# Index columns copied one at a time on GpSimd, each beside its own gather

## The chip, the cores and the metric

One NeuronCore of one Trainium2 chip runs the program. The metric is the device time of one execution in microseconds (us), the median of the runs shown; lower is better. TensorE is called PE here, VectorE DVE, ScalarE ACT, GpSimd POOL and SyncE SP.

## The reference

A chain of four graph layers over 100000 nodes of 64 float32 features and 50000 edges. Each layer takes `h = relu(layernorm(x))` and adds its result to `x`:

```python
edge_index = jnp.stack([src, dst])
h = jnp.maximum(_layernorm(x), 0.0)
x = x + _L0_gnn_ref(h, edge_weight, edge_index, 2)      # two weighted hops: segment_sum(w * x[src], dst)
h = jnp.maximum(_layernorm(x), 0.0)
x = x + _L1_gnn_ref(h, edge_index, W, b)                # degree-normalised convolution
h = jnp.maximum(_layernorm(x), 0.0)
x = x + _L2_gnn_ref(h, edge_index, W1, b1, W2, b2)      # neighbour sums, then a two-layer MLP
h = jnp.maximum(_layernorm(x), 0.0)
x = x + _L3_gnn_ref(h, src, dst, edge_attr_32, ...)     # messages of both end nodes and edge features, MLP, sum, MLP
```

## The kernel before

The edges are sorted by destination. They lie in SBUF with 128 partitions and T = 392 columns (391 edges of a partition and one for its border). A unit is G = 14 columns, there are U = 28 units, and a step is a pair of units, b = 0 and 1, so there are STEPS = 14 steps. Rows of 64 features that belong to one column are fetched or written by one indirect DMA of POOL: 128 rows of 256 bytes, with 128 row numbers, one in each partition. So a unit costs 14 indirect DMAs, a step 28.

The program has five stages, one after the other, in each of which all engines work on the same steps:

- the first hop (`hop0` on POOL): POOL gathers rows of `x` and scatters sums with an add into two tables. The gathers of the first four units are issued ahead of everything, in the loop over `u` at the top of the diff; the later ones stand between the scatters and take their row numbers from slots that DVE fills. Those later ones are not touched
- the second hop (`hop1`): POOL scatters with an add into `xu`, 28 DMAs in a step, and gathers nothing
- the first and the second source pass, called S0 and S1 below (`for k, f in enumerate(sp_)`, the function `body`): POOL gathers 28 columns a step, from `xu` in S0 and from `tables[0]` in S1. At the same time the other engines also work through all 100000 nodes (the dense pass), independent of these gathers except for their place in each engine's order
- the last pass, called T below (`t_gather`, `t_scatter`): in a regular step POOL first scatters the 28 columns of one step to `out` and then gathers the 28 columns of the step three further on. DVE's side is `last_pass`.

Each engine has one instruction order, written out by hand, and engines wait on semaphores. The row numbers of a gather are read from a slot, `isl[b]`, a tile of 128x14 int32, and not from the large index tile. `slot_copy` is the copy of POOL that fills a slot and raises `s_slot`; `gather` then issues one indirect DMA for each column. In S0 a slot and its buffer `ga[b]` are free when DVE has centred the rows of that unit (`centred`, L2251); in S1 when DVE has added them to another tile (`ga_free`, L2227). In T DVE itself fills the slot for the next gather (`next_slots`, L2382) and only then raises `ga_free`; POOL fills it only for the first step. POOL scatters of step i (L1059) wait for `o_ready`, which DVE raises late in its pass (the profile shows it as "DVEq L80"), and every following gather of POOL stands behind them in its order.

Of the kernel before, what the change touches and what calls it, by code (L numbers as in the profile page):

```python
# [14 lines left out]
G = 14  # L15
U = T // G
STEPS = U // 2
# [140 lines left out]
def gnn(nc, x, src, dst, edge_attr, edge_weight, W1g, b1g, W2a, b2a, W2b, b2b, mW1, mb1, mW2, mb2, uW1, ub1,  # L158
        uW2, ub2, out):
    ctx = ExitStack()  # L160
    with ctx:
# [10 lines left out]
        tables = [dram(f"table{k}", [ROWS + P, D]) for k in range(2)]  # L172
# [49 lines left out]
        dstc_i = sb("dstc_i", [P, T], I32)  # L222
        ptr_i = sb("ptr_i", [P, T], I32)
# [15 lines left out]
        hin, xw, h, vt, ga = (pair(n, unit) for n in ("hin", "xw", "h", "vt", "ga"))  # L239
# [5 lines left out]
        us = pair("us", unit)  # L245
# [24 lines left out]
        isl, osl = (pair(n, [P, G], I32) for n in ("isl", "osl"))  # L270
        isl_of = [*isl, *pair("isl_ahead", [P, G], I32)]
# [18 lines left out]
        ga_of = [*(t[:, :, :] for t in ga), ccu[0][2], ccu[1][2]]  # L290
# [90 lines left out]
        s_slot = sem("pool_slot_copied")  # L381
# [26 lines left out]
        B2K = [0, 1]  # L408
# [451 lines left out]
        def _(pool):  # L860
# [62 lines left out]
            def slot_copy(o, i_):  # L923

                return nc.gpsimd.tensor_copy(o, i_).then_inc(s_slot, 1)

            def gather(o, table, idx, s, columns=range(G)):
                for g in columns:
                    nc.gpsimd.indirect_dma_start(  # L929
                        o[:, g, :], None, table, bass.IndirectOffsetOnAxis(idx[:, g:g + 1], 0)).then_inc(s, 16)  # L930


            after.wait_ge(s_node, 1)
            base = 0

            hop_max, all_max = pool.to_reg(ROWS + 4 * P - 1), pool.to_reg(ROWS + N + 4 * P - 1)
            f = hops[0]
            for u in range(4):  # L940
                slot_copy(isl_of[u][:, :], dstc_i[:, u * G:u * G + G])
                after.wait_ge(s_slot, base + u + 1)
                gather(ga_of[u], x, isl_of[u], f.got[u])
            base += 4

            def hop0(i):
                for b in B2K:
# [60 lines left out]
            for k, f in enumerate(sp_):  # L1008
                if k == 0:
                    table, index = xu, u_i  # L1010
                else:
                    table, index = tables[k - 1], ptr_i
                    for b in B2K:
                        after.wait_ge(sp_[0].kept[b], 2 * 16 * STEPS)

                def body(i, first):
                    for n, b in enumerate(B2K if k == 0 else B2K[::-1]):
                        if not first:

                            if k == 0:  # L1020
                                after.wait_ge(*f.centred.at(i - 1, ("l", b)))
                            else:
                                after.wait_ge(*f.ga_free.at(i - 1, ("g", b)))
                        slot_copy(isl[b][:, :], index[:, bass.ds(ecol(i, b), G)])
                        after.wait_ge(s_slot, base + 2 * i + n + 1)
                        gather(ga[b], table, isl[b], f.got[b])

                for i in range(STEPS):
                    body(i, i == 0)
                base += 2 * STEPS  # L1030
# [12 lines left out]
            def t_gather(i, first=False):  # L1043
                for b in B2K:
                    if not first:
                        after.wait_ge(*tt.ga_free.at(i - 1, ("g", b)))
                    if first:
                        slot_copy(isl[b][:, :], ptr_i[:, bass.ds(tcol(i, b), G)])
                        after.wait_ge(s_slot, base + b + 1)
                    gather(ga[b], tables[1], isl[b], tt.got_a[b])  # L1050

            def t_scatter(i, first=False):
                for b in B2K:
# [8 lines left out]

            for q in LANES:
                after.wait_ge(s_dense[q], 16 * DSTEPS)
            t_gather(0, True)
            t_gather(1)
            t_gather(2)
            t_scatter(0, True)
            t_gather(3)
            for i in range(2, STEPS - 2):  # L1070
                t_scatter(i - 1)
                t_gather(i + 2)
            for i in (STEPS - 3, STEPS - 2):
                t_scatter(i)

# [681 lines left out]
        def _(dve):  # L1757
# [619 lines left out]

            descending = range(G - 1, -1, -1)

            def next_slots(n, b):  # L2380
                n = 0 if isinstance(n, int) and n == STEPS else n
                return V.tensor_copy(isl[b][:, :], ptr_i[:, bass.ds(tcol(n, b), G)])  # L2382

            def last_pass(i, first=False, more_steps=True):
                if i is not None:
                    own.step(i)
# [47 lines left out]
                if more_steps:  # L2434
                    hd = layer_norm(own, tt, j, "d1", B2K, [full(gx[b]) for b in B2K], [full(xw[b]) for b in B2K],
                                    [[(tt.load_x[b], 32 * (j + 1))] for b in B2K],
                                    scale=lambda b: dis_d[:, bass.ds(tcol(j, b), G)])
                    for b in B2K:
                        own.wait(hd[b], (tt.load[b], 16 * 6 * (j + 1)))
                        hd[b] = own.did(V.tensor_tensor(full(xw[b]), full(xw[b]), full(a3[b]), ALU.add))  # L2440
                    for b in B2K:
                        own.wait(hd[b])
                        settled(dve, j)
                        tt.rows.raise_by(V.tensor_tensor(full(xw[b]), full(xw[b]), cols(dis_d, tcol(j, b)), ALU.mult), ("vd", b))

                    for b in B2K:
                        own.wait((tt.got_a[b], 16 * G * (j + 1)))
                        tt.rows.raise_by(V.tensor_tensor(full(us[b]), full(hin[b]), full(ga[b]), ALU.add), ("us", b))
                    for b in B2K:
                        next_in = own.did(next_slots(j + 1, b))  # L2450
                        own.wait(tt.rows.at(j, ("us", b)), next_in)
                        tt.ga_free.raise_now(dve, ("g", b))

                aggregate(0)
# [122 lines left out]
            def first_step():  # L2577
# [69 lines left out]
                    own.wait((tt.got_a[b], 16 * G), (tt.load[b], 16 * 6))  # L2647
                    tt.rows.raise_by(V.tensor_tensor(full(us[b]), full(hin[b]), full(ga[b]), ALU.add), ("us", b))
                for b in B2K:
                    next_in = own.did(next_slots(1, b))  # L2650
                    own.wait(tt.rows.at(0, ("us", b)), next_in)
# [66 lines left out]
```

## Time and profile before

| | |
|---|---|
| median of 3 runs | 4624.67 us (4622.48 to 4624.89) |
| span of the profiled execution | 5754.7 us |
| span minus median | 1130.0 us |
| first hop and what is ahead of it | 0 to about 1210 us |
| second hop | about 1210 to 2130 us |
| S0 | about 2130 to 3068 us |
| S1 | about 3068 to 4002 us |
| T | about 4002 us to the end |
| indirect DMAs of POOL | 2760 of its 2843 instructions |

The profiled execution's only time is its span; nothing is given for it outside the span. It is longer than the runs that are timed, so a duration in it is read as that of a profiled execution, and where the two must differ is a question of its own. In the rows, "idle before" is the time in which an engine did nothing before an instruction, and the name behind the arrow is what released it: "issue" is nothing that the profile shows, "remote" an update for which the profile has no instruction that ended at that time.

### The profile page before, as it was taken

The numbers are of one execution on the slowest core, as the hardware profiler recorded it, in microseconds if no ns is written. First come the engines' busy times: TensorE is split into PE (matmuls) and PEld (weight loads), VectorE is DVE, ScalarE is ACT, GpSimd is POOL, SyncE is SP. The second block draws the span as 40 slices with busy tenths as digits, with TensorE's granted clock in tenths as the row PEclk, the third lists the DMA queues.
The fourth block names the chain that finished last, engine by engine and source line by source line (L and its number), as shares of the span: only waits on it lengthen the run. The fifth ranks groups of instructions, "written<-read, shape, count | busy, mean of one in ns | idle before, by whom it ended". The sixth has DMA issues, their size and how long they took to land. (4 is left out here: it accounts for less than half of the span.)

```text
span 5754.7 us, 60611 instructions
## 1 busy us (share of the span) xinstructions
PE 3759.0 (65%) x18706; PEld 3006.2 (52%) x18706; DVE 3033.3 (53%) x7288; ACT 2016.3 (35%) x5132; POOL 3313.7 (58%) x2843
## 2 busy tenths in 40 slices
PE   3776666676999975565556777763566655666665
PEld 2544444446898964444445555553454444455454
DVE  4644444455556546665665766755454434455442
ACT  2444444451111113443444444431233333333332
POOL 4888888887888874444332554553444554445544
PEclk7776666675555557887888777875778877777787
DMA  8333333334444432222222333333121111121110
GB/s 293 51 51 51 51 51 51 51 42 73 87 81 87 87 40 82 78 93 79 96 77 75 108 125 123 112 107 130 54 91 55 59 57 57 54 91 55 60 54 21
DMA packets 335488, 452.10 MB, mean 79 GB/s; under 512 B 208111, under 2 KB 233301, under 8 KB 334740
## 3 DMA queue, kind: packets, MB, share of 16 engines
q1 hardware_dynamic: 159268, 361.69, 17.8%
q0 software_dynamic: 176000, 87.72, 12.5%
q8 instruction: 109, 1.79, 0.1%
q14 instruction: 111, 0.91, 0.1%
HBM read 258.41 MB, written 225.53 MB: 84 GB/s over the span
## 5 line engine op out<-in xcount | busy, mean ns | idle before, releaser
L929 POOL DMA_INDIRECT ga<-table,isl x784 | 783.9, 1000 | 278.1 <-issue 231.3
L1059 POOL DMA_INDIRECT out_x<-acc,osl x392 | 430.0, 1097 | 755.6 <-DVEq L80 640.4
L997 POOL DMA_INDIRECT xu<-acc,osl x392 | 625.1, 1595 | 144.6 <-issue 103.1
L1205 PE MATMUL tp<-xw,cc 128*128 128x394 f32 x784 | 411.5, 623 | 345.8 <-DVE cc L2011 215.4
L1242 PE MATMUL tp<-us,wide 128*128 128x64 f32 x1568 | 416.8, 422 | 87.4 <-DVE us L2139 49.2
L929 POOL DMA_INDIRECT ga<-xu,isl x392 | 394.0, 1005 | 121.5 <-issue 116.5
L1205 PEld LDWEIGHTS tp<-xw,cc 128*128 128x128 f32 x784 | 141.5, 220 | 603.1 <-issue 325.4
L1093 PE MATMUL mm<-ident,wide 128*128 128x128 f32 x1176 | 213.1, 343 | 355.6 <-DVE wide L2218 275.7
L1242 PEld LDWEIGHTS tp<-us,wide 128*128 128x128 f32 x1568 | 380.0, 332 | 92.2 <-DVE us L2139 49.4
L1255 PE MATMUL tp<-acc,wide 128*128 128x64 f32 x1560 | 423.3, 427 | 0.8
L1093 PEld LDWEIGHTS mm<-ident,wide 128*128 128x128 f32 x1176 | 180.0, 182 | 406.1 <-issue 323.2
L1255 PEld LDWEIGHTS tp<-acc,wide 128*128 128x128 f32 x1560 | 372.0, 329 | 20.8 <-ACT acc L1558 5.6
L1190 PE MATMUL tp<-us,wide 128*128 128x64 f32 x1568 | 341.0, 421 | 59.0 <-DVE us L1928 59.0
L960 POOL DMA_INDIRECT hop_even<-acc,osl x196 | 321.9, 1642 | 99.5 <-issue 57.3
L1190 PEld LDWEIGHTS tp<-us,wide 128*128 128x128 f32 x1568 | 336.6, 332 | 64.8 <-issue 64.8
L960 POOL DMA_INDIRECT hop_odd<-acc,osl x196 | 321.6, 1641 | 60.8 <-issue 57.3
L1558 ACT ACTIVATE acc<-tp,h 128x64 f32<-128x64 f32 x392 | 102.0, 311 | 691.7 <-PE tp L1255 536.6
L2461 DVE SCALAR_TENSOR_TENSOR mean_row<-st,mm 128x14 f32<-128x14 f32 x26 | 4.4, 168 | 587.3 <-remote 549.1
L1128 PE MATMUL mm<-bias,rows 128*128 128x455 bf16 x392 | 158.7, 405 | 228.2 <-issue 77.0
L1100 PE MATMUL mm<-cc,u1s 128*128 128x512 f32 x448 | 249.9, 691 | 76.0 <-ACT zx L1593 50.5
L1523 ACT ACTIVATE hin<-tp,xw 128x391 bf16<-128x391 f32 x392 | 233.1, 595 | 133.7 <-PE tp L1205 88.3
L1093 PE MATMUL tp<-ident,us 128*128 128x128 f32 x392 | 75.1, 360 | 312.3 <-ACT eft L1697 257.0
(378 smaller groups left out, 9513.8 us busy)
## 6 DMA issues: line engine op xcount, KB each, us to landing
wide<-xu SPq DMA_DIRECT2D x84, 448.0 KB
zx<-key_rows SPq DMA_DIRECT2D x28, 896.0 KB
out_x<-wide SPq DMA_DIRECT2D x56, 448.0 KB, 3.4
table<-acc SPq DMA_DIRECT2D x56, 448.0 KB, 2.5
xf<-xs SPq DMA_DIRECT2D x56, 448.0 KB
wide<-table SPq DMA_DIRECT2D x56, 448.0 KB
xu<-in_x SPq DMA_DIRECT2D x25, 1000.0 KB
hop_even<-zeros SPq DMA_DIRECT2D x1, 12544.0 KB
```

What stands on the lines that cost most here:

```text
L929: nc.gpsimd.indirect_dma_start(o[:, g, :], None, table, bass.IndirectOffsetOnAxis(idx[:, g:g + 1], 0)).then_inc(s, 16)
L960: nc.gpsimd.indirect_dma_start(hop[odd], bass.IndirectOffsetOnAxis(osl[b][:, g:g + 1], 0), acc[b][:, g, :], None, compute_op=ALU.add).then ...
L997: nc.gpsimd.indirect_dma_start(xu, bass.IndirectOffsetOnAxis(osl[b][:, g:g + 1], 0), acc[b][:, g, :], None, compute_op=ALU.add).then_inc(f ...
L1059: nc.gpsimd.indirect_dma_start(out, bass.IndirectOffsetOnAxis(osl[b][:, g:g + 1], 0), acc[b][:, g, :], None, bounds_check=nodes_max, oob_i ...
L1093: t = nc.tensor.transpose(o[0:w, j * P:j * P + P], blk, ident[:, :])
L1100: t = nc.tensor.matmul(o[:, c:c + n], weights, flat(src_)[:, c:c + n], start=True, stop=extra is None)
L1128: nc.tensor.matmul(o[:, at:at + HB * C], rows3[:, :], bias[:, k, 0:HB * C], start=True, stop=False)
L1190: t = nc.tensor.matmul(o[:, g * D:g * D + D], equal[b][:, c, (g % 2) * P:(g % 2) * P + P], us[b][:, c, :], start=n == 0, stop=n == 1)
L1205: f.key_row.raise_by(nc.tensor.matmul(tp[1][:, at:at + KEYS], reach[:, g * P:g * P + P], key_steps, start=True, stop=True), ("g", b, g))
L1242: t = nc.tensor.matmul(o, equal_run[:, 2 * q + n, mine:mine + P], us[b][:, 2 * q + n, :], start=n == 0, stop=alone and n == 1)
L1255: t = nc.tensor.matmul(o, equal_run[:, c, 2 * P + mine:3 * P + mine], passed[:, c, :], start=False, stop=n == 1)
L1523: nc.scalar.activation(sign_out[:, 2 * (g % 2), 0:EC], tp[1][:, at + 3:at + KEYS], ACT.Sign, bias=key_high[:, column], scale=-1.0, accum_o ...
```

## The change

A new helper, `gather_by_column`, takes the place of the pair of one slot copy and one `gather` of 14 columns. For each column g it copies one column of the index tile (128x1) into column g of the slot, waits until that copy has raised `s_slot`, and issues the gather of that column. It serves the four units ahead of the first hop, S0, S1 and all of T. In T POOL now copies for every step, so DVE's `next_slots` copies (28 of them) and its wait on them go away; `ga_free` still waits for DVE's sum. The number of gathers, their order, their tables and their buffers stay as they are.

```diff
+            def gather_by_column(o, table, slot, index, c, s, copied):
+                for g in range(G):
+                    slot_copy(slot[:, g:g + 1], index[:, c + g:c + g + 1])
+                    after.wait_ge(s_slot, copied + g + 1)
+                    gather(o, table, slot, s, (g,))
+                return copied + G
...
             for u in range(4):
-                slot_copy(isl_of[u][:, :], dstc_i[:, u * G:u * G + G])
-                after.wait_ge(s_slot, base + u + 1)
-                gather(ga_of[u], x, isl_of[u], f.got[u])
-            base += 4
+                copied = gather_by_column(ga_of[u], x, isl_of[u], dstc_i, u * G, f.got[u], copied)
...
-                        slot_copy(isl[b][:, :], index[:, bass.ds(ecol(i, b), G)])
-                        after.wait_ge(s_slot, base + 2 * i + n + 1)
-                        gather(ga[b], table, isl[b], f.got[b])
+                        copied = gather_by_column(ga[b], table, isl[b], index, ecol(i, b), f.got[b], copied)
...
-            def t_gather(i, first=False):
+            def t_gather(i, copied, first=False):
                 for b in B2K:
                     if not first:
                         after.wait_ge(*tt.ga_free.at(i - 1, ("g", b)))
-                    if first:
-                        slot_copy(isl[b][:, :], ptr_i[:, bass.ds(tcol(i, b), G)])
-                        after.wait_ge(s_slot, base + b + 1)
-                    gather(ga[b], tables[1], isl[b], tt.got_a[b])
+                    copied = gather_by_column(ga[b], tables[1], isl[b], ptr_i, tcol(i, b), tt.got_a[b], copied)
+                return copied
...
-            def next_slots(n, b):
-                n = 0 if isinstance(n, int) and n == STEPS else n
-                return V.tensor_copy(isl[b][:, :], ptr_i[:, bass.ds(tcol(n, b), G)])
...
                     for b in B2K:
-                        next_in = own.did(next_slots(j + 1, b))
-                        own.wait(tt.rows.at(j, ("us", b)), next_in)
+                        own.wait(tt.rows.at(j, ("us", b)))
                         tt.ga_free.raise_now(dve, ("g", b))
```

## Rows read from the trace of the kernel before

**Rows 1.** The page: the span.

```profile
span 5754.7 us, 60611 instructions
```

**Rows 2.** Groups of POOL's instructions by line: busy us, mean ns, idle before.

```profile
L929 POOL DMA_INDIRECT ga<-table,isl x784 | 783.9, 1000 | 278.1 <-issue 231.3 <-DVEq L80 39.8 <-POOL isl L925 7.1
L925 POOL COPY isl<-ptr_i 128x14 int32<-128x14 int32 x30 | 9.4, 312 | 352.0 <-DVE us L2227 349.4 <-DMA table<-fix 2.5
L925 POOL COPY isl<-map_idx 128x14 int32<-128x14 int32 x28 | 6.3, 225 | 339.5 <-DVE xc L2251 338.3 <-DMA xu<-hsum 1.2
...
L2707 POOL MEMSET const-float32-0.0<- 128x1 f32 x1 | 0.1, 104 | 0.3 <-issue 0.3
```

**Rows 3.** Whom DVE waited for, in S0, S1 and T: us, times, longest.

```profile
DVE mean_row L2208 <- remote: 191.3, 14, 20.4
DVE wide L2218 <- remote: 76.2, 11, 16.1
...
DVE wide L2218 <- remote: 151.7, 12, 13.7
DVE xw L2240 <- remote: 38.8, 8, 14.9
...
DVE mean_row L2461 <- remote: 549.1, 20, 48.6
```

**Rows 4.** Stretches of ten steps of S0, ten of S1, eight of T.

Columns: stretch, length, then busy us (instructions) of PE, PE's weight loads, DVE, ACT and POOL, granted PE clock, DMA share, GB/s.

```profile
2309.00:2953.00 644.00, 368.81 (x1982) 282.48 (x1981) 405.88 (x721) 266.73 (x561) 284.42 (x301) 0.80 0.27 86
3231.00:3846.00 615.00, 448.25 (x2480) 356.59 (x2480) 425.27 (x721) 285.12 (x582) 301.41 (x300) 0.80 0.36 119
4444.00:5428.00 984.00, 585.85 (x3504) 476.97 (x3504) 455.76 (x960) 339.06 (x625) 461.89 (x448) 0.78 0.20 63
```

**Rows 5.** POOL in order of time, S0, between the two units of a step.

```profile
2327.37 0.94 POOL L929 DMA_INDIRECT ga<-xu,isl  x1 [0.30 <-issue]
2328.31 0.21 POOL L925 COPY isl<-map_idx 128x14 int32<-128x14 int32 x1
2328.80 0.98 POOL L929 DMA_INDIRECT ga<-xu,isl  x1 [0.27 <-issue]
```

**Rows 6.** The same place in S1: DVE's instruction and POOL's copy.

```profile
3188.49 1.09 DVE L2200 SCALAR_TENSOR_TENSOR wide<-wide,st 128x896 f32<-128x896 f32 x1
...
3189.17 0.46 POOL L925 COPY isl<-ptr_i 128x14 int32<-128x14 int32 x1
```

**Rows 7.** Around the end of one gather burst of T, in order of time.

```profile
4886.77 0.95 POOL L929 DMA_INDIRECT ga<-table,isl  x1 [0.30 <-issue]
4894.19 0.17 DVE L2461 SCALAR_TENSOR_TENSOR mean_row<-st,mm 128x14 f32<-128x14 f32 x1 [8.73 <-remote]
4936.12 1.64 POOL L1059 DMA_INDIRECT out_x<-acc,osl  x1 [48.40 <-DVEq L80]
```

**Rows 8.** One burst of S0 with DVE's next start; first copy of one of S1.

```profile
2309.04 0.20 POOL L925 COPY isl<-map_idx 128x14 int32<-128x14 int32 x1 [24.23 <-DVE xc L2251]
2345.84 0.95 POOL L929 DMA_INDIRECT ga<-xu,isl  x1 [0.30 <-issue]
2349.48 1.09 DVE L2218 TENSOR_TENSOR wide<-wide,mm 128x896 f32<-128x896 f32 x1 [11.28 <-remote]
...
3231.24 0.20 POOL L925 COPY isl<-ptr_i 128x14 int32<-128x14 int32 x1 [23.66 <-DVE us L2227]
```

**Rows 9.** Late in T: the first scatter after a step without a gather burst.

```profile
5637.43 1.61 POOL L1059 DMA_INDIRECT out_x<-acc,osl  x1 [44.36 <-DVEq L80]
```

**Rows 10.** Ahead of the first hop: two DVE instructions, then POOL's first scatter.

```profile
89.86 1.28 DVE L2011 TENSOR_SCALAR cc<-mm,small 128x1024 f32<-128x1024 f32 x1 [28.24 <-remote]
104.62 1.02 DVE L2011 TENSOR_SCALAR cc<-mm,small 128x768 f32<-128x768 f32 x1 [13.48 <-remote]
138.23 1.63 POOL L960 DMA_INDIRECT hop_even<-acc,osl  x1 [40.13 <-ACT acc L1536]
```

**Rows 11.** DVE's slot copies in T: ns min/median/max, first and last start.

```profile
L2382 DVE COPY isl<-ptr_i x28: 163/171/175, 4058.2 to 5574.1; 128x14 int32<-128x14 int32 x28
```

More of the change, by code:

```diff
@@ L930, in gather @@
                         o[:, g, :], None, table, bass.IndirectOffsetOnAxis(idx[:, g:g + 1], 0)).then_inc(s, 16)
+            def gather_by_column(o, table, slot, index, c, s, copied):
[4 more added lines that the diff above has]
+                return copied + G
             after.wait_ge(s_node, 1)
-            base = 0
+            copied = 0
             hop_max, all_max = pool.to_reg(ROWS + 4 * P - 1), pool.to_reg(ROWS + N + 4 * P - 1)
@@ L1014, in _, with body @@
                         after.wait_ge(sp_[0].kept[b], 2 * 16 * STEPS)
-                def body(i, first):
-                    for n, b in enumerate(B2K if k == 0 else B2K[::-1]):
+                def body(i, first, copied):
+                    for b in B2K if k == 0 else B2K[::-1]:
                         if not first:
@@ L1023, in body @@
                                 after.wait_ge(*f.ga_free.at(i - 1, ("g", b)))
-                        slot_copy(isl[b][:, :], index[:, bass.ds(ecol(i, b), G)])
-                        after.wait_ge(s_slot, base + 2 * i + n + 1)
-                        gather(ga[b], table, isl[b], f.got[b])
+                        copied = gather_by_column(ga[b], table, isl[b], index, ecol(i, b), f.got[b], copied)
+                    return copied
                 for i in range(STEPS):
-                    body(i, i == 0)
-                base += 2 * STEPS
+                    copied = body(i, i == 0, copied)
                 for b in B2K:
@@ L1046, in t_gather @@
                         after.wait_ge(*tt.ga_free.at(i - 1, ("g", b)))
-                    if first:
-                        slot_copy(isl[b][:, :], ptr_i[:, bass.ds(tcol(i, b), G)])
-                        after.wait_ge(s_slot, base + b + 1)
-                    gather(ga[b], tables[1], isl[b], tt.got_a[b])
+                    copied = gather_by_column(ga[b], tables[1], isl[b], ptr_i, tcol(i, b), tt.got_a[b], copied)
+                return copied
             def t_scatter(i, first=False):
@@ L1064, in _ @@
                 after.wait_ge(s_dense[q], 16 * DSTEPS)
-            t_gather(0, True)
-            t_gather(1)
-            t_gather(2)
+            copied = t_gather(0, copied, True)
+            copied = t_gather(1, copied)
+            copied = t_gather(2, copied)
             t_scatter(0, True)
-            t_gather(3)
+            copied = t_gather(3, copied)
             for i in range(2, STEPS - 2):
                 t_scatter(i - 1)
-                t_gather(i + 2)
+                copied = t_gather(i + 2, copied)
             for i in (STEPS - 3, STEPS - 2):
@@ L2649, in first_step @@
                 for b in B2K:
-                    next_in = own.did(next_slots(1, b))
-                    own.wait(tt.rows.at(0, ("us", b)), next_in)
+                    own.wait(tt.rows.at(0, ("us", b)))
                     tt.ga_free.raise_now(dve, ("g", b))
```

## Prediction

> **What bounds the kernel now.** I read the page for the span, then POOL's groups by line, then the waits of DVE, then stretches of regular steps, and last single bursts in order of time. The first thing to see is that the profiled execution is not the timed one: its span is 5754.7 us [rows 1], the median of the runs 4624.67 us, 1130.0 us less. What the change costs depends on which time is missing from the timed runs.
>
> Two readings close that gap. By the first, DVE's waits on "remote" are in the profiled execution alone. They come to 267.5 us in S0, 190.5 us in S1 and 549.1 us in T [rows 3], together 1007 us, and 5754.7 - 1007 = 4748 us, within 123 us of the median. In each of these waits no instruction in the profile ended when DVE went on; DVE goes on only when POOL's burst of gathers has ended: 6.5 us after it in T (the last gather ends at 4887.72, DVE starts at 4894.19) [rows 7], 2.7 us after it in S0 (2346.79 to 2349.48) [rows 8]. I call such a wait a hold. By the second reading the holds are in the timed runs too, and POOL is quicker there: 1130 / 2760 indirect DMAs = 0.41 us each, of the 1.25 us that one takes from start to start. The first is likelier, since it needs one effect of a size that the trace itself shows, and the second needs a third off every DMA.
>
> Without holds a regular step is shorter. S0: 644 / 10 = 64.4 us [rows 4] less 267.5 / 14 = 19.1 us gives 45.3 us, with DVE busy for 40.6 us. S1: 61.5 less 190.5 / 14 = 13.6 gives 47.9 us, with DVE busy for 42.5 us. T: 984 / 8 = 123.0 us less 549.1 / 11 = 49.9 us (eleven steps have a gather burst beside a full pass) gives 73.1 us, with PE busy for 73.2 us and DVE for 57.0 us. POOL works in a step of T for 123.0 - 48.4 = 74.6 us, and waits for DVE's `o_ready` in the rest [rows 7]. So without holds POOL is as late as the others in T. Against this stands the one step of T that has a full pass and no gather burst: POOL's scatters take 39.4 us (74.6 less a gather burst of 35.0, 28 by 1.25) and it then waits 44.36 us [rows 9], 83.8 us in all, in which the other engines were not held. The step of T in the timed runs lies between 74.6 and 83.8 us. As the timed median is 123 us below my sum without holds, I take it near the low end, 75.6 us.
>
> In the two hops POOL has the longest work, but their inner gathers are not changed.
>
> **The price of one column.** Before, a gather follows another after 0.95 + 0.30 = 1.25 us. Where a slot copy stands between two gathers, the copy starts the moment the gather ends, takes 0.21 us, and the next gather starts 0.27 us after it: 2328.80 - 2327.37 = 1.43 us [rows 5]. The new code makes this pattern at every column, so a column costs 0.18 us more. The trace shows no copy of 128x1. From below, a POOL instruction of 128x1 takes 0.104 us [rows 2], which would leave 0.18 - 0.11 = 0.07 us. From above, a copy that stood beside a two-operand instruction of DVE took 0.46 us and ended when DVE's did (3189.63 and 3189.58) [rows 6]: 0.43 us more for such a column. The copies from `map_idx` average 0.225 us and those from `ptr_i` 0.312 us [rows 2], so where DVE is busy I use 0.28 us as the upper price. I take 0.18 us, as copies that meet nothing take 0.2 us with 14 columns, and the fixed part is most of it.
>
> The Trainium skill ("SBUF — State Buffer", section "SBUF: two separate sides") speaks against this change: a GpSimd instruction that reads SBUF and a DVE instruction with two SBUF inputs take the same port pair as an exclusive lock, and the later one blocks until the first is through. The copy of 0.46 us agrees. By that rule each of the some 1170 new copies is a new occasion to stand behind DVE, and if all did, the price would be that of rival 3.
>
> **Part by part.**
>
> 1. Ahead of the first hop: 56 columns by 56 copies in place of 4, so 52 by 0.18 = 9.4 us on POOL. The first scatter comes at 138.23, 40.13 us after the early gathers ended at 98.10; but 28.24 and 13.48 us of DVE's time ahead of it are holds, of which the second ends at 104.62, 6.5 us after POOL's burst [rows 10]. Without these 41.7 us the sums for the scatter would be there at 96.5, before POOL is free. So POOL's burst is on the path there, and the hop after it is POOL's own: +9.4 us.
>
> 2. S0: 28 copies a step in place of 2, 26 by 0.18 = 4.7 us, at 0.28 us 7.3 us. POOL's burst is 2309.04 to 2346.79, 37.8 us, and I let the rows be in place 2.7 us later, at the latest when DVE went on [rows 8]: 40.5 us of a step of 45.3. What hides the change is this 4.8 us; it is used up at 0.18 us and short by 2.5 us at 0.28 us. If it is short, `source_mean` of DVE is late, and the dense pass behind it in DVE's order too. Between 0 and 2.5 by 13 steps = 33 us; I take 0.8 us a step, 10 us.
>
> 3. S1: the burst is 61.5 - 23.7 = 37.8 us [rows 4, 8], with 2.7 us 40.5 of 47.9: 7.4 us of cover for 4.7 to 7.3 us. Taken as 0.
>
> 4. T: DVE's 28 copies of 0.17 us [rows 11] go, and 28 copies a step on POOL come, 5.0 us at 0.18 us. POOL's wait on a copy holds up its gathers, and behind them the scatters of the next step. POOL's step goes from 74.6 to 79.6 us; from a step of 75.6 us that is +4.0 us, by 11 steps +44 us. At a step of 83.8 us it is nothing. The three early gather bursts of T have POOL waiting for DVE behind them, so they are hidden. `ga_free` is raised some 0.3 us sooner, for nothing as DVE then waits for ACT's and PE's products anyway; where DVE or PE is the bound it is a gain of at most 28 by 0.17 = 4.8 us.
>
> Semaphore traffic and DMA: no transfer is added, and the gathers are the same ones in the same order.
>
> Sum: 9.4 + 10 + 0 + 44 = 63 us; 4624.67 + 63 = 4688 us. Against the profiled execution, where the holds end with the bursts, everything is serial: 9.4 + 13 by 4.7 twice (122) + 11 by 5.0 (55) = 187 us, with 0.28 us in S0 and S1 254 us. The span should be 5942 to 6009 us.
>
> **Rivals.**
>
> 1. Hidden. The step of T is near 83.8 us, or POOL is a little quicker when not profiled (0.07 us a DMA would account for 110 of the 123 us in the two hops alone). For it: the unheld step of rows 9. Against it: the sum of rows 3, which the median undercuts. Time: 4624.67 within 9 us, 0.2%, which is about what a measurement of this kernel can tell from no change.
>
> 2. The holds are real in the timed runs. Then every burst is on the path, as in the profile: +187 to +254 us, 4812 to 4879 us. For it: the holds end so strictly with the bursts. Against: a third off every DMA of POOL.
>
> 3. Most copies stand behind DVE, 0.43 us a column. S0: 26 by 0.43 = 11.2 less 4.8 cover, by 13 = 83 us; S1: 11.2 less 7.4, by 13 = 49 us; T: 74.6 + 12.0 - 75.6 = 11.0 by 11 = 121 us; with 52 by 0.43 = 22 us ahead, +275 us, 4900 us. Against: the copies of S0 that met DVE's reduces took 0.20 us.
>
> 4. Faster. If holds are real, they come with the rate at which gathers are issued: 28 gathers at 1.43 us instead of 1.25 us are a rate 13% lower. A hold of 49.9 us a step of T that shrinks by 13% gives back 6.5 us for the 5.0 us that the burst is longer: it decides from 10% on. By 11 steps -17 us, with the same in S0 and S1 (19.1 and 13.6 us a step, where it does not pay) at best a fall of the whole to about 4600 us. For it: holds appear only under dense gathers. Against: in the hops, where POOL never pauses, PE goes on nonetheless.
>
> **Chances.** The forecast (some 10 to 120 us slower) 0.50; hidden 0.27; rival 2 0.10; rival 3 0.04; faster 0.09. The point is the forecast's own, 4688 us. The range reaches from 4612 us, which holds the hidden case with a small gain, to 4790 us, which holds the T step at 0.28 us a column (74.6 + 7.8 - 74.6 by 11 = 86 us), S0's 33 us, S1's few us and the 15 us ahead (52 by 0.28). Left out are rivals 2 and 3 and two thirds of the faster case, 0.20. The forecast's own range is 4635 to 4745 us. Faster by over 0.2% 0.09; within 0.2% 0.22, since a part of the hidden case still pays the 9.4 us ahead of the first hop; slower 0.69.
>
> **What the changed kernel's profile would show.** Copies of 128x1 of about 0.2 us, over 1230 of them; from gather to gather 1.43 us in T and 1.45 to 1.55 us in S0 and S1; T's regular step 128 us, with POOL's wait before L1059 still 48 us; S0's and S1's steps 5 to 8 us longer; no L2382-like copy on DVE. If POOL's waits shrink by what its bursts grow, the price is hidden even there, and rival 1 is right. If DVE's "remote" waits shrink, rival 4 has its mechanism. Wrong would make me above all a copy of one column that is much cheaper or dearer than 0.2 us, and a step of T in the timed runs that POOL does not set.

## The result, and the profile after

The changed kernel takes 4806.07 us (median of 4 runs, 4793.73 to 4812.52), the kernel before 4624.78 us (4 runs): a ratio of 1.0388 [1.0372, 1.0404], 181 us slower. The forecast was 4688 us, slower, in 4612 to 4790 us. The sign held; the time lies above the range.

The page of the kernel after: span, busy time, and the chain that ended last.

```profile
span 4791.4 us, 61753 instructions
...
PE 3584.7 (75%) x18706; PEld 2876.9 (60%) x18706; DVE 3036.1 (63%) x7260; ACT 2010.5 (42%) x5132; POOL 3707.0 (77%) x4013
...
POOL 40%; issue 13%; PE 8%; DVE 6%; DMA 3%; ACT 1%; DVEq 0%; SPq 0%; POOLq 0%; ACTq 0%
```

The span is 963 us shorter than that of [rows 1], though the kernel is slower. No DVE wait on "remote" as in [rows 3] is left, and POOL no longer waits for `o_ready` in the steps of T (the 48.40 us of [rows 7] are gone). So this profile can't be laid beside the profile before. What it needs is an execution of the unchanged stages without those waits; the run `only_ahead` below gives one.

POOL's groups of the kernel after: busy us, mean ns, idle before. They answer to [rows 2].

```profile
L929 POOL DMA_INDIRECT ga<-table,isl x784 | 825.2, 1053 | 224.7 <-POOL isl L925 212.8
...
L929 POOL DMA_INDIRECT ga<-xu,isl x392 | 426.8, 1089 | 111.9 <-POOL isl L925 106.5
...
L925 POOL COPY isl<-ptr_i 128x1 int32<-128x1 int32 x784 | 225.5, 288 | 43.1 <-DVE us L2228 32.3
```

POOL's instructions on `isl` in the kernel after: ns min/median/max.

```profile
L925 POOL COPY isl<-ptr_i x784: 181/194/1132, 2825.4 to 4623.7; 128x1 int32<-128x1 int32 x196
```

POOL of the kernel after in order of time: in S1, with the instruction of DVE that the copy meets, then in T, undisturbed. They answer to [rows 5, 6].

```profile
3018.20 1.09 DVE L2201 SCALAR_TENSOR_TENSOR wide<-wide,st 128x896 f32<-128x896 f32 x1
3018.32 1.01 POOL L925 COPY isl<-ptr_i 128x1 int32<-128x1 int32 x1
3019.61 0.97 POOL L929 DMA_INDIRECT ga<-table,isl  x1 [0.27 <-POOL isl L925]
...
4253.87 1.01 POOL L929 DMA_INDIRECT ga<-table,isl  x1 [0.27 <-POOL isl L925]
4254.89 0.19 POOL L925 COPY isl<-ptr_i 128x1 int32<-128x1 int32 x1
4255.35 0.97 POOL L929 DMA_INDIRECT ga<-table,isl  x1 [0.27 <-POOL isl L925]
```

The undisturbed pattern is the one foreseen: a gather of 0.97 to 1.01 us, a copy of 0.19 us, 0.27 us idle, 1.45 to 1.48 us for a column. The mean is another matter. The median copy takes 194 ns and the mean copy 288 ns: some take up to 1.13 us. In S0, S1 and T 188 of the 1176 copies take over 0.3 us, and each of these ends within 0.08 us of the end of a DVE instruction that reads two tiles in SBUF, as the one at 3018.32 does (3019.33 and 3019.29). Beside a DVE instruction of the same length whose second input is `mm`, which TensorE wrote, a copy stays short; this is one of 77 such copies, in S0:

```profile
2128.69 1.08 DVE L2211 TENSOR_TENSOR wide<-wide,mm 128x896 f32<-128x896 f32 x1
2129.29 0.19 POOL L925 COPY isl<-map_idx 128x1 int32<-128x1 int32 x1
```

### The profile page after: what moved, and what is told of

Its sections match the earlier page's. It is cut to its first block, busy times and chain, and to the rows that moved or that the text cites. A ratio compares the mean times of both kernels' runs of the same rounds, so it can differ in the third digit from the quotient of the medians.

```text
span 4791.4 us, 61753 instructions
## 1 busy us (share of the span) xinstructions
PE 3584.7 (75%) x18706; PEld 2876.9 (60%) x18706; DVE 3036.1 (63%) x7260; ACT 2010.5 (42%) x5132; POOL 3707.0 (77%) x4013
## 4 chain that ended last, share of the span: by engine, by line
POOL 40%; issue 13%; PE 8%; DVE 6%; DMA 3%; ACT 1%; DVEq 0%; SPq 0%; POOLq 0%; ACTq 0%
POOL ga L929 22%; POOL out_x L1060 9%; POOL isl L925 6%; POOL xu L1002 4%; PE tp L1256 2%; PE tp L1243 2%; DMA xu<-acc,osl 2%; PE mm L1101 2%; PE mm L1120 1%; DVE xf L1945 1%; DVE wide L2104 1%; DVE acc L1945 1%; PE mm L1132 1%; PE mm L1094 0%; DVE wide L2099 0%
## 5 line engine op out<-in xcount | busy, mean ns | idle before, releaser
L929 POOL DMA_INDIRECT ga<-table,isl x784 | 825.2, 1053 | 224.7 <-POOL isl L925 212.8
L929 POOL DMA_INDIRECT ga<-xu,isl x392 | 426.8, 1089 | 111.9 <-POOL isl L925 106.5
L1101 PE MATMUL mm<-cc,u1s 128*128 128x512 f32 x448 | 215.7, 608 | 104.3 <-ACT zx L1594 83.0
L1094 PE MATMUL mm<-ident,wide 128*128 128x128 f32 x1176 | 191.6, 314 | 109.6 <-DVE wide L2201 59.9
L1537 ACT COPY acc<-tp 128x896 f32<-128x896 f32 x28 | 25.3, 905 | 574.9 <-DMA hop_even<-acc,osl 287.4
L925 POOL COPY isl<-ptr_i 128x1 int32<-128x1 int32 x784 | 225.5, 288 | 43.1 <-DVE us L2228 32.3
L1094 PEld LDWEIGHTS mm<-ident,wide 128*128 128x128 f32 x1176 | 161.5, 167 | 148.8 <-DVE wide L2201 79.1
```

The source lines that it names most:

```text
L929: nc.gpsimd.indirect_dma_start(o[:, g, :], None, table, bass.IndirectOffsetOnAxis(idx[:, g:g + 1], 0)).then_inc(s, 16)
L1094: t = nc.tensor.transpose(o[0:w, j * P:j * P + P], blk, ident[:, :])
L1101: t = nc.tensor.matmul(o[:, c:c + n], weights, flat(src_)[:, c:c + n], start=True, stop=extra is None)
```

## The experiments

In the kernels below the line numbers are some ten higher than in the kernel after. They ran on four chips, and the chips fall into two kinds. On two the unchanged kernel takes 4620 to 4624 us, as it did beside the result above; on the other two it takes 5829 and 5831 us, in timed runs. I call them quiet chips and holding chips. One of the quiet chips was used at two times and was quiet at both; no holding chip was, so it is likely, and not shown, that the chip decides and not the moment. The unchanged kernel's runs on the same chip stand beside each result.

### The unchanged kernel on a holding chip (control)

> The kernel before, unchanged, for its profile. Theory 1 (the holds on DVE belonged to that one profiled execution): a span of about 4622 us, near its time, T's regular step 76 us. Theory 2 (the profiled execution of this kernel always has them, and the column copies take them away): a span near 5755 us.

5820.14 us, with a span of 5817.8 us; the median of 13 runs there is 5828.88 us. Whom DVE waited for:

```profile
DVE mean_row L2461 <- remote: 512.1, 12, 49.9
DVE mean_row L2208 <- remote: 269.7, 15, 23.4
...
DVE wide L2218 <- remote: 125.3, 23, 12.5
```

These are the holds of [rows 3], in an execution whose span and time agree within 3 us. On a quiet chip the two agree as well (span 4618.7 us of 4621.03 us, next experiment). So profiling neither makes the holds nor lengthens the run, and neither theory is right as it was put: the span is long, but the timed runs there are as long. The profile before most likely came from a holding chip and its timed runs from a quiet one; which chip it was isn't recorded.

### One stage at a time, on quiet chips

The kernel before, with `gather_by_column` in one place only and this in the others; in `only_t` also without DVE's slot copies:

```diff
+            def gather_unit(o, table, slot, index, c, s, copied):
+                slot_copy(slot[:, :], index[:, c:c + G])
+                after.wait_ge(s_slot, copied + 1)
+                gather(o, table, slot, s)
+                return copied + 1
```

> The column copies only in the four units ahead of the first hop, 14-column copies elsewhere. Theory 1 (POOL's early burst is on the path): 52 more copies at some 0.18 us, +9 us, about 4634 us. Theory 2 (the first scatter waits for the other engines anyway): 4625 us.

> The column copies only in S0. Theory 1 (POOL is the bound of a step in S0 when the kernel is timed, and a column costs what the changed kernel's trace shows, 1.64 us from gather to gather in place of 1.31): up to 28 x 0.33 = 9 us a step, less what slack there was; +45 to +100 us. Theory 2 (the prediction's: DVE sets the step of S0, POOL has 4.8 us of cover): +10 us or less.

> The column copies only in S1. Theory 1 (as in S0): +40 to +90 us. Theory 2 (the prediction's: 7.4 us of cover in a step): 0 us.

> The column copies only in the last pass, DVE's slot copies gone. Theory 1 (POOL's 28 scatters and 28 gathers set the step, which is 83.5 us in the changed kernel against some 76 us): +70 to +90 us. Theory 2 (S0 and S1 cost nothing, so all of the +181 us is here): +165 to +175 us.

> The column copies in S0 and S1 alone, the rest as before. On a chip without holds: the sum of the two measured alone, +38 and +48, so +86 us, if the stages are independent. On a chip with holds: theory 1 (wider spaced gathers end the holds of S0 and S1 completely, as in the trace of the changed kernel there): 14 steps by 18 us and 14 by 14 us less, some -430 us, 5400 us, with T's 125 us a step as before. Theory 2 (what ends them is elsewhere, in T's move of the copy from DVE): within 2% of the kernel before.

| | us | before | ratio | us more | forecast |
|---|---|---|---|---|---|
| only_ahead | 4622.18 | 4624.43 | 1.0000 [0.9990, 1.0009] | 0 | 9.4 |
| only_s0 | 4662.26 | 4624.43 | 1.0085 [1.0068, 1.0102] | 38 | 10 |
| only_s1 | 4672.25 | 4624.43 | 1.0106 [1.0089, 1.0123] | 48 | 0 |
| only_t | 4713.72 | 4624.43 | 1.0200 [1.0183, 1.0217] | 89 | 44 |
| s0_and_s1 | 4711.42 | 4622.67 | 1.0190 [1.0177, 1.0204] | 89 | 10 |

The four single stages sum to 175 us of the 181. S0 and S1 together cost what they cost alone (38 + 48 = 86). Of what was expected before these runs, S1's and T's theory 1 held; S0's theory 1 was too high (at least 45, measured 38), and ahead of the first hop theory 2 held. The trace of `only_ahead` serves from here as the profile of the stages before: its S0, S1 and T are unchanged, and its time is.

Regular steps of S0 (5), S1 (8) and T (6) in `only_ahead`; columns as in [rows 4], to which they answer:

```profile
2423.30:2645.70 222.40, 170.52 (x992) 130.72 (x991) 201.96 (x361) 133.04 (x281) 152.37 (x150) 0.92 0.39 125
2957.20:3312.80 355.60, 305.10 (x1984) 247.74 (x1984) 336.62 (x577) 226.19 (x465) 251.36 (x240) 0.96 0.50 166
3845.10:4300.90 455.80, 403.53 (x2639) 326.58 (x2639) 343.92 (x722) 253.91 (x469) 353.39 (x336) 0.95 0.33 101
```

The same of the kernel after: 4, 8 and 6 steps.

```profile
2397.00:2585.00 188.00, 137.93 (x794) 106.08 (x793) 163.25 (x289) 106.29 (x226) 153.11 (x224) 0.90 0.37 118
3053.80:3435.00 381.20, 317.30 (x1984) 260.25 (x1984) 340.42 (x577) 227.52 (x464) 315.97 (x448) 0.92 0.47 153
3874.80:4375.80 501.00, 408.19 (x2633) 329.05 (x2631) 342.79 (x710) 253.47 (x470) 400.17 (x505) 0.91 0.30 92
```

A step goes from 44.5 to 47.0 us in S0, from 44.4 to 47.6 us in S1, from 76.0 to 83.5 us in T. POOL's busy time in a step of T goes from 58.9 to 66.7 us, 7.8 us for a step that is 7.5 us longer; DVE's stays at 57 us. PE's clock falls a little, from 0.95 to 0.91 of full speed; PE's busy time in a step of T grows by less than 1 us, so this is not what the step waits for.

Two of POOL's groups in `only_ahead`, and below them two of its waits (us, times, longest):

```profile
L929 POOL DMA_INDIRECT ga<-table,isl x784 | 815.0, 1040 | 247.9 <-issue 230.2 <-DVEq L80 9.6 <-POOL isl L925 8.1
...
L971 POOL DMA_INDIRECT hop_even<-acc,osl x196 | 321.9, 1642 | 81.5 <-issue 56.1 <-DMA xu<-ga 22.1 <-ACT acc L1546 3.4
```

```profile
POOL isl L925 <- DVE us L2237: 94.0, 13, 43.6
...
POOL isl L925 <- DVE xc L2261: 66.5, 12, 8.0
```

Whom DVE waited for in the kernel after (in `only_ahead` these two come to 11.9 us in 2 waits and 2.4 us in one):

```profile
DVE us L2228 <- DMA ga<-table,isl: 52.7, 13, 15.8
...
DVE st L2245 <- DMA ga<-xu,isl: 36.9, 13, 8.6
```

The direction has turned. Before, POOL waited for DVE's buffer once a step: 66.5 / 12 = 5.5 us in S0, and (94.0 - 43.6) / 12 = 4.2 us in S1 without the first. That is the cover, and after the change it is used up: DVE waits for the gathers in every step.

The price of a column comes out of the two groups of `table` gathers, per gather: 1.053 - 1.040 more for the gather, (224.7 - 247.9) / 784 = -0.030 for the idle time before it, and 0.288 for the copy, together 0.27 us. Of this, 0.19 - 0.03 + 0.03 (a gather of 974 ns in the median in place of 944) is the undisturbed 0.19 us; the rest, near 0.08 us, comes from copies that were stretched to as much as 1.13 us. The stages differ: the mean copy takes 276 ns in S0, 327 ns in S1 and 248 ns in T. A step's 28 gathers with what stands between them, from the start of the first to the end of the last (median of twelve steps), go from 38.7 to 46.0 us in S0, from 39.5 to 47.4 us in S1 and from 35.9 to 43.8 us in T.

Ahead of the first hop the 52 copies are hidden. In `only_s1`, where that part is unchanged, the first scatter's group reads:

```profile
L971 POOL DMA_INDIRECT hop_even<-acc,osl x196 | 321.5, 1640 | 90.8 <-issue 56.1 <-DMA xu<-ga 31.4 <-ACT acc L1546 3.4
```

Its wait for stored rows ("DMA xu<-ga") is 31.4 us there and 22.1 us in `only_ahead`: the 9.3 us are what POOL's burst has grown.

### The copy's place and number, on a quiet chip

All are the kernel after with another helper. `copies_first_3` issues 14 copies of one column, then one wait, then the 14 gathers. `copy_ahead_3` issues the copy of the next column ahead of a gather, so a gather waits for an older copy:

```diff
+                for g in range(G + 1):
+                    if g < G:
+                        slot_copy(slot[:, g:g + 1], index[:, c + g:c + g + 1])
+                    if g:
+                        after.wait_ge(s_slot, copied + g)
+                        gather(o, table, slot, s, (g - 1,))
```

`copied_twice` makes each copy a second time into a tile that nothing reads (two lines of its loop, set against those of `gather_by_column`):

```diff
                     slot_copy(slot[:, g:g + 1], index[:, c + g:c + g + 1])
+                    slot_copy(second_slot[:, g:g + 1], index[:, c + g:c + g + 1])
-                    after.wait_ge(s_slot, copied + g + 1)
+                    after.wait_ge(s_slot, copied + 2 * g + 2)
```

`t_pool_unit` uses `gather_unit` everywhere: one copy of 14 columns, made by POOL in T too. `direct_3` has no slots at all in the places of the change; the gathers read `index[:, c + g:c + g + 1]`.

> The 14 copies of 128x1 of a unit first, one wait, then its 14 gathers; wanted for a chip where the kernel before takes 4624 us. Theory 1 (the copy's own time on POOL is the price): +100 us or more. Theory 2 (the chain of copy, semaphore and gather at every column is the price): +50 us or less. On a chip with holds: about 5580 us, as before.

> The copy for column g + 1 ahead of the gather of column g; wanted for a chip where the kernel before takes 4624 us. Theory 1 (the copy's own time is the price): +170 us, as the changed kernel. Theory 2 (the wait on it is about half of the price): +60 to +110 us. On a chip with holds: about 5555 us.

> The changed kernel with a second copy of 128x1 at each column, of the same row numbers into a tile that nothing reads; the gather waits for both. On a chip without holds: theory 1 (a copy costs its own 0.19 us and waits behind DVE, POOL is the bound in S0, S1 and T): 1232 more copies, some 0.1 to 0.2 us each, +110 to +240 us on the changed kernel, 4920 to 5050 us. Theory 2 (the semaphore round trip is the price and a second copy passes under it): within 60 us of the changed kernel. On a chip with holds: S0 and S1 longer by the copies, T's holds shorter again, or not, if the rate of the gathers has nothing to do with them.

> 14-column copies everywhere, as before, but in T they are POOL's for every step in place of DVE's. On a chip without holds: theory 1 (POOL sets T's step): 2 x 0.18 us by 11 to 14 steps, +4 to +6 us, the part of +89 us that comes from moving the copy to POOL. Theory 2 (the move to POOL itself is dear, the gather waits there for a copy behind the scatters): +20 us or more. On a chip with holds: within 1% of the kernel before.

> No slots in the changed places, the gathers take their row numbers from the index tile. On a chip without holds: theory 1 (a gather costs the same from either tile; S0 and S1 have some 5 us a step in which POOL waits for DVE, so their slot copies were hidden, and T had them on DVE): within 9 us of the kernel before. Theory 2 (POOL's copies in S0 and S1 are paid): -10 us. On a chip with holds, as measured twice: the time of the kernel before.

| | us | before | ratio | us more | step of T |
|---|---|---|---|---|---|
| direct_3 | 4620.57 | 4622.67 | 0.9997 [0.9988, 1.0006] | 0 | 76.1 |
| t_pool_unit | 4630.88 | 4620.39 | 1.0022 [1.0013, 1.0032] | 10 | 77.5 |
| copy_ahead_3 | 4712.62 | 4620.39 | 1.0198 [1.0181, 1.0215] | 92 | 80.9 |
| copies_first_3 | 4720.76 | 4620.39 | 1.0219 [1.0202, 1.0236] | 100 | 82.1 |
| after | 4806.07 | 4624.78 | 1.0388 [1.0372, 1.0404] | 181 | 83.5 |
| copied_twice | 4955.62 | 4620.39 | 1.0728 [1.0710, 1.0746] | 335 | 88.0 |

The step of T is the mean of six, from first scatter to first scatter. Of what was expected, theory 1 held for `copies_first_3`, `copied_twice` and `direct_3` and theory 2 for `copy_ahead_3`; `t_pool_unit` fell between its two.

POOL in order of time, T: `copies_first_3`, then `copy_ahead_3`, then `copied_twice`.

```profile
4263.74 2.45 POOL L925 COPY isl<-ptr_i 128x1 int32<-128x1 int32 x14
4266.46 1.00 POOL L929 DMA_INDIRECT ga<-table,isl  x1 [0.27 <-POOL isl L925]
4267.76 0.96 POOL L929 DMA_INDIRECT ga<-table,isl  x1 [0.30 <-issue]
```

```profile
4271.72 0.19 POOL L925 COPY isl<-ptr_i 128x1 int32<-128x1 int32 x1
4272.07 0.97 POOL L929 DMA_INDIRECT ga<-table,isl  x1 [0.15 <-POOL isl L925]
```

```profile
4253.28 0.21 POOL L926 COPY isl<-ptr_i 128x1 int32<-128x1 int32 x1
4253.45 0.17 POOL L926 COPY second_slot<-ptr_i 128x1 int32<-128x1 int32 x1
4253.89 0.97 POOL L930 DMA_INDIRECT ga<-table,isl  x1 [0.27 <-POOL second_slot L926]
```

Fourteen copies back to back take 2.45 us, 0.175 us each, and one wait of 0.27 us serves 14 gathers. Made so, the copies cost 100 us of the 181. The other 81 us are what it adds to have each copy beside its own gather. These are the two groups of `copies_first_3` to set beside those of the kernel after:

```profile
L929 POOL DMA_INDIRECT ga<-table,isl x784 | 824.8, 1052 | 237.5 <-issue 222.3 <-POOL isl L925 15.2
...
L925 POOL COPY isl<-ptr_i 128x1 int32<-128x1 int32 x784 | 139.9, 234 | 54.0 <-DVE us L2242 48.2 <-DVEq L80 3.2 <-DMA table<-fix 2.5
```

The gathers take the same, 824.8 and 825.2 us, and POOL's idle time before them is even shorter in the kernel after (224.7 us in place of 237.5; 247.9 in `only_ahead`): the wait behind each copy takes the place of the 0.30 us that lie between two gathers anyway. The copies differ: the same 784 keep POOL busy for 225.5 us one by one and for 139.9 us in rows of 14 (the mean of 234 ns counts the overlap of neighbours twice). 188 copies take over 0.3 us in the kernel after and 74 here, a row of 14 giving DVE one occasion to be in its way and single copies fourteen.

Taking the gather off its own copy (`copy_ahead_3`) cuts the idle time from 0.27 to 0.15 us, below the usual 0.30 us, and the cost to 92 us, though 212 of its copies take over 0.3 us. A second copy of each column adds another 335 - 181 = 154 us, 0.125 us for each of the 1232. `direct_3` says what the slots are worth on a quiet chip: nothing, neither way. So no version here beats the kernel before there. Moving the copy of 14 columns from DVE to POOL in T costs 10 us by itself: POOL's copies from `ptr_i` come to 19.1 us in `t_pool_unit` and to 9.3 us in `only_ahead`.

### The same kernels on holding chips

`copies_first`, `copy_ahead` and `direct` are the kernels just described, run twice each; `after_again` is the changed kernel.

> Everywhere where the changed kernel copies by column: the 14 copies of 128x1 of a unit first, one wait, then its 14 gathers. As many copies, no wait between them. Theory 1 (the price of a column is the copy's own time on POOL, some 0.2 to 0.3 us, wherever it stands): about 4800 us, as the changed kernel. Theory 2 (the price is that a copy, its semaphore and the next gather form one chain at every column, which leaves nothing of the 0.30 us between two gathers to hide in): copies back to back take perhaps 0.1 us each, so some 1.4 us a unit in place of 3.9: 4680 us or less.

> As the changed kernel, but the copy for column g + 1 is issued ahead of the gather of column g, so that the gather's wait has been met long before. Theory 1 (the copy's own time is the price): about 4800 us. Theory 2 (the wait is the price: the gather can't be issued until the copy's update has come back): the copy sits in the 0.30 us between two gathers and the kernel comes back to 4625 to 4700 us.

> No slots in the changed places: each gather takes its 128 row numbers from the column of the index tile itself (the places are written out, so their columns are constants). Same rows gathered. Theory 1 (POOL is the bound in T, and a unit's 14-column copy costs 0.18 us there only if POOL does it): within 10 us of the kernel before. Theory 2 (a gather that reads a column of a tile with 392 columns is slower than one that reads a slot): slower by some 1230 x the difference.

> The 14 copies of 128x1 of a unit first, one wait, then its 14 gathers; wanted on a chip where the kernel before takes 4624 us. Theory 1 (the copy's own time on POOL is the price, 0.19 us by 14 in place of one of 0.2): 1204 copies, in T 28 by 0.19 = 5.3 us a step and nearly as much in S0 and S1, so +100 us or more. Theory 2 (the chain of copy, semaphore and gather is the price): copies back to back at 0.1 us, +50 us or less.

> The copy for column g + 1 ahead of the gather of column g; wanted on a chip where the kernel before takes 4624 us. In the trace of the other chip the gathers of T then follow each other in 1.37 us, against 1.24 there and 1.43 by the changed kernel's pattern. Theory 1 (the copy's own time is the price): +170 us as the changed kernel. Theory 2 (half of the price is the wait): +60 to +110 us.

> No slots in the changed places, the gathers take their row numbers from the index tile; wanted on a chip where the kernel before takes 4624 us. Theory 1 (a gather costs the same from either tile; POOL is the bound in T, where the kernel before has no copies on POOL): within 9 us of the kernel before. Theory 2 (POOL is the bound in S0 and S1 too): 26 to 28 steps with 2 copies less at 0.18 us, -10 us.

> The changed kernel itself, beside the kernel before on one chip. In the four runs before this the kernel before took 5829 us on another chip, with the holds of its first profile, against 4624 us. Theory 1 (there are chips with holds and chips without; the price of the change is POOL's only where there are none): where the kernel before takes 4624 us, +181 us; where it takes 5829 us the rarer gathers shorten the holds, and the changed kernel is faster, some 5500 to 5600 us. Theory 2 (the two times are a matter of the moment and not of the chip): both kernels change together within the rounds.

| | us | before | ratio |
|---|---|---|---|
| direct | 5830.93 | 5828.88 | 0.9996 [0.9974, 1.0019] |
| direct_2 | 5832.59 | 5830.65 | 1.0004 [0.9987, 1.0022] |
| copies_first | 5590.62 | 5828.88 | 0.9580 [0.9530, 0.9630] |
| copies_first_2 | 5578.91 | 5830.65 | 0.9577 [0.9555, 0.9598] |
| copy_ahead | 5552.06 | 5828.88 | 0.9519 [0.9486, 0.9552] |
| copy_ahead_2 | 5555.22 | 5830.65 | 0.9530 [0.9507, 0.9552] |
| after_again | 5234.99 | 5830.65 | 0.8986 [0.8965, 0.9006] |

On such a chip the change makes the kernel 10% faster, 5235 us where theory 1 expected 5500 to 5600. Taking the slots away does nothing here either, and copies in rows of 14 already gain 4%, but hardly in T: there, with the gathers of a unit still 1.25 us apart, the steps of `copies_first` are 122.8 us, and those of `copy_ahead`, 1.39 us apart, 124 to 126 us, against 123 to 125 us in `control`. Their gain is in S0 and S1 (from the first gather to the border sum `hsum`, from 943 and 933 us in `control` to 801 and 893 us in `copies_first`, 849 and 780 us in `copy_ahead`). Whom DVE waited for in `after_again`; no other hold is among its ten longest waits:

```profile
DVE mean_row L2457 <- remote: 350.1, 20, 40.5
```

Steps of S0 (2), S1 (8) and T (9) in `after_again`, columns as in [rows 4]:

```profile
2404.00:2499.50 95.50, 69.43 (x397) 53.69 (x397) 81.43 (x145) 53.09 (x113) 75.66 (x112) 0.89 0.37 116
3072.20:3459.80 387.60, 318.30 (x1989) 260.40 (x1990) 341.56 (x578) 226.36 (x464) 322.33 (x448) 0.92 0.45 150
3845.60:4898.40 1052.80, 660.45 (x3942) 534.07 (x3942) 511.06 (x1063) 382.37 (x703) 578.76 (x756) 0.80 0.22 66
```

A step of S0 is 47.8 us here and 64.4 us in [rows 4], of S1 48.5 and 61.5 us: near the steps of a quiet chip (47.0 and 47.6 us). A step of T is 117 in place of 123 us, 105 to 108 us in every third and 122 to 123 us in the others; there the holds are only shorter. In T the gathers are mostly 1.43 us apart, 1.49 us on average; in S0 and S1, with DVE beside them, 1.63 and 1.73 us. This distance is in part a result: where DVE isn't held, it works beside POOL and stretches the copies.

What a hold is can be read from one place in T. In `only_ahead` on a quiet chip, PE's last matmul of a unit and DVE's next instruction:

```profile
4396.88 0.33 PE L1143 MATMUL mm<-wg,vt 128*128 128x65 f32 x2
...
4397.24 0.17 DVE L2471 SCALAR_TENSOR_TENSOR mean_row<-st,mm 128x14 f32<-128x14 f32 x1 [0.59 <-PE mm L1143]
```

The same in `control` on a holding chip, with the first and the last gather of POOL's burst:

```profile
4903.48 0.99 POOL L929 DMA_INDIRECT ga<-table,isl  x1 [0.30 <-issue]
4918.99 0.33 PE L1133 MATMUL mm<-wg,vt 128*128 128x65 f32 x2
4937.24 0.95 POOL L929 DMA_INDIRECT ga<-table,isl  x1 [0.30 <-issue]
4944.88 0.17 DVE L2461 SCALAR_TENSOR_TENSOR mean_row<-st,mm 128x14 f32<-128x14 f32 x1 [45.66 <-remote]
```

DVE goes on 0.03 us after the matmul in the one and 25.6 us after it in the other. It waits for one semaphore, which only TensorE raises, and the trace of `control` has that update at 4944.86, 0.02 us before DVE starts. So DVE isn't slow to notice: what tells it that TensorE is through comes late. This holds for TensorE's results alone: in the same burst TensorE itself goes on 0.06 us after ACT's `vt` (4915.59 and 4915.65). ACT's waits of this kind in `control`:

```profile
ACT vt L1496 <- remote: 282.4, 34, 18.0
...
ACT xf L1674 <- remote: 166.4, 30, 15.4
ACT zx L1593 <- remote: 132.9, 23, 15.7
```

All instructions of DVE and ACT that were held read `mm` or `tp`, which TensorE writes, and PE, POOL and SP, which wait for the other engines, have no "remote" row at all. Whether TensorE finishes late (the profile only models the ends of its matmuls) or finishes in time and its update is late, no run here tells apart. TensorE also has idle times in `control` that the profile puts down to nothing (ahead of L1133 alone 19, 32.2 us in all); in `only_ahead` it has none in these stages.

## Why the prediction was wrong

**The two readings of the gap** (first reading, holds not in the timed runs). Right for the timed chip, with a wrong reason: `control` shows the holds in timed runs of their own. The second reading falls: in `only_ahead` a median gather takes 0.944 us, what it took in [rows 5]; POOL is not quicker anywhere.

**The hold-free steps.** S0 was put at 45.3 us and is 44.5; T at 75.6 and is 76.0, POOL-bound without a gap, as chosen. S1 was put at 47.9 us and is 44.4. For S1 I took off only the largest "remote" rows of DVE; ACT's holds, and what a late engine costs the others, stayed in.

**The price of one column.** This step failed first. I took 0.18 us; the mean is 0.27 us. The undisturbed 0.19 us was right, and the stretched copies were put at nothing, though the bound of 0.28 us from the mean of the copies [rows 2] stood beside it. It should have been the value: in steps that DVE fills to 57 of 76 us (T) or 42 of 44 us (S1), copies meet it. The Trainium skill ("SBUF — State Buffer", "SBUF: two separate sides") has a GpSimd instruction that reads SBUF and a DVE instruction with two SBUF inputs exclude each other, so that the later one blocks until the first is through; the 188 copies of over 0.3 us that end with such an instruction, up to 1.13 us beside a median of 0.194 us, and the short copies beside adds from `mm` agree with that. Rival 3, all copies behind DVE at 0.43 us, was too much: 188 of 1176 were.

**The cover in S0 and S1.** This step failed as well. The bursts were put at 37.8 us, taken from steps in which DVE stood still, and take 38.7 us in S0 and 39.5 us in S1 when DVE works beside them (28 gathers at 1.38 and 1.41 us). With the shorter step, S1's cover was 4.2 us of POOL's idle time and not 7.4. The bursts grow by 7.9 us a step in S1 and 7.3 us in S0. S1: 7.9 - 4.2 = 3.7 us by 13 = 48 us, as measured; S0: 7.3 - 5.5 = 1.8 by 13 = 23 us, measured 38. In `only_s0` the first step of S0, which has no cover, is 5.6 us longer than in `only_ahead`; the other 9 us or so of S0 I have not resolved.

**Ahead of the first hop.** +9.4 us forecast, 0 measured. DVE's holds were rightly struck out, but the next to be late there is the store of gathered rows, which the hop waits for until 22.1 us after POOL is free. With the holds in the trace, that wait didn't show.

**T.** Mechanism right: 7.5 us a step by 11 = 83 us and 89 us for the stage, in place of 44; the term was mis-sized by the column's price (28 by 0.27 = 7.6 us). Moving the copies from DVE to POOL, +10 us in `t_pool_unit`, is in it.

So 9.4 + 10 + 0 + 44 = 63 should have read 0 + 38 + 48 + 89 = 175 us. My own bounds at 0.28 us a column, 33 us in S0 and 86 us in T, are close to what was measured. The terms named for the upper end of the range come to 33 + 86 + 15 = 134 us and a "few us" for S1; S1's 48 us are what it lacked.

**The rivals.** Rival 1, hidden: wrong, but for the part ahead of the hop. Its 110 us by a quicker POOL was also too much: the two hops have 1176 indirect DMAs, at 0.07 us 82 us. Rival 2 gives 4812 us, near the measured 4806.07 us, by another way: it has real holds and no cover, and on the timed chips there are no holds and a real cover. Rival 4, holds that shrink with the gather rate, was priced at 17 us and judged from T alone. On a holding chip it is the largest effect of all, 596 us. From the first gather of the stage to its border sum (`hsum`), S0 takes 943 us in `control` and 694 us in `after_again`, S1 933 and 735 us: 447 of the 586 us between the two spans, where I had written that it doesn't pay. I had let a hold shrink in proportion to the rate; in fact, at 1.6 to 1.7 us a gather it is all but gone.

**The profile of after.** Copies of 0.2 us, 1232 of them, 1.43 us a column in T: right where nothing is beside them; the means from gather to gather are 1.56 us in T and 1.65 and 1.71 us in S0 and S1, where 1.45 to 1.55 was forecast. The sign named for rival 4, DVE's "remote" waits shrinking, did come true in `after_again`, with 350.1 us in T in place of 549.1. Span of 5942 to 6009 us, step of T of 128 us, POOL's wait of 48 us: wrong, even for the kind of chip that they were meant for, where the span is 5231.6 us and the step of T 117 us.

## What to carry to other kernels

Before a profile is used to explain a time, ask whether the two can be of the same execution; here they differed by 1130 us, which was more than any edit was worth, and an unchanged kernel run once with a profile would have shown which waits were real. A small copy in front of every item of a stream costs most where the stream's engine has no idle time: price it by the mean of like instructions beside a busy neighbour, not by the undisturbed one, and take the cover as the idle time of that engine in a profile where all engines run. Here a cover of a tenth of the step did not hide it. Where such copies are needed, make them in a row ahead of the items: here that took the cost from 181 to 100 us.

## What the hardware showed that I had not expected

The same program takes 4624 us on some chips and 5830 us on others, 26% more, each steady within some tenths of a per cent, and the same edit is 3.9% slower on the one kind and 10.1% faster on the other. On the second kind DVE and ACT learn late that TensorE has finished while POOL issues gathers every 1.25 us, 25.6 us late in the place shown; what the other engines raise comes in time: no wait on them is "remote" in `control`. With gathers 1.6 to 1.7 us apart on average these holds are all but gone, at 1.49 us apart they are shorter. Spacing is not all of it: `copies_first` has breaks of some 2.7 us between units, and most of its 4% is gained in S0 and S1, while in T, with the same breaks, its steps are 122.8 us in place of 123 to 125. `direct` shows that the slots as such have no part in it. Why breaks and spacing help, and what is different on those chips, no run here settles; the rate of the gathers' descriptors and that of their completions were not told apart.
